# Ten FFN tiles ahead of the experts instead of twelve, sums through a PSUM bank

## The chip, the cores and the metric

The kernel runs on one core of a Trainium2 chip, in one launch. The metric is the device time of one execution in microseconds; of several runs the median is taken. The core has TensorE (PE in the profile, its weight loads PEld), VectorE (DVE), ScalarE (ACT), GpSimd (POOL) and SyncE (SP), each with its own queue of instructions in order, and they wait for each other on semaphores. All matrix products go to PSUM, which has eight banks of 512 fp32 columns on 128 partitions.

## The reference

A pre-norm decoder layer on x of 32 sequences x 64 rows x 256, that is 2048 rows or 16 tiles of 128. Linear attention and cross attention come first; the change lies in the FFN. There every row gets a shared FFN of width 352 and the two best of eight experts of width 176:

```python
x = x + linear_attention(_layernorm(x))
x = x + cross_attention(_layernorm(x), ctx)
xf = _layernorm(x)
weights, indices = top_k(softmax(xf @ gate_w.T), 2)      # weights over their sum
out = sum over the two experts e: weight_e * (silu(xf @ w_gate[e]) * (xf @ w_up[e])) @ w_down[e]
sh = silu(xf @ shw_gate) * (xf @ shw_up) @ shw_down
x = x + out + sigmoid(xf @ shgate_w) * sh
```

## The kernel before, in words

A tile is 128 rows. The attention loop works on 16 tiles in a software pipeline; its last tiles are drained by hand among the first shared FFN tiles. Every product of the FFN is three fp32r matmuls (high times high, high times low, low times high; `product`, L833), for which ScalarE writes the high half of an operand and VectorE the low one.

**A shared tile t.** TensorE transposes x_send (`transpose_sx`, L840); ScalarE writes s_xh, VectorE s_xl (`shared_x_low`, L1646). Then `shared_gate` and `shared_up` (12 matmuls), tanh on ScalarE (L1189), two VectorE steps (`s_gg` L1652, `s_h` L1657, together `shared_h`), three transposes (`transpose_sh`, L877), the split into s_hh (L1194) and s_hl (`sh_low`, L1662), nine matmuls (`shared_down`) and the addition to x_all (`residual3`, L1669). There is one down bank, DN, so `shared_down(t)` waits for `residual3(t-1)`.

**Routing.** VectorE ranks the rows in two batches, BATCHES = tiles 0 to 9 and 10 to 15. GpSimd then sends each tile by two indirect DMAs (`send`, L514) to rows in DRAM that are sorted by expert. Sends are paced by waits on s_h or e_h.

**The experts.** 39 slots of 128 sorted rows. SyncE loads slot i to xs (L410); the first FULL_SLOTS = 13 slots need batch 0 alone (semaphore sent0), and slots 4 to 11 have a clearing write behind each (L404). For slot i TensorE does `transpose_slots`, `gate_up` (6 matmuls), `transpose_h` (L972) and `expert_down` (6 matmuls), of different slots in one turn of the loop. ScalarE weights the result into e_y (`copy_y`, L1264, a ring of four), and GpSimd scatters it to y_rows (`scatter_out`, L568).

**Order.** It is written out by hand for each engine. EARLY_SHARED = 12 shared tiles run ahead of the experts, four behind them. The first two late tiles are mixed with the last two expert products: gate and up of tile 12 come ahead of `expert_down(37)`, and those of tile 13 behind `expert_down(38)`.

**The end.** When all scatters have landed, SyncE loads y_rows back as eight yg pieces of 512 KB, two tiles each (L427). GpSimd adds the two rows of each (`sum_y`, L577), VectorE adds the sum to x_all (`combine`, L1815), SyncE stores (L434). All eight combines stand on VectorE behind `sh_low(15)` and ahead of `residual3(14)`:

```python
while t >= TILES and done < PAIRS:
    combine(done)
    done += 1
if t >= TILES:
    v.wait_ge(sm["comb_ready"], PAIRS)
residual3(t - 2)
```

## Time and profile before

| | us |
|---|---|
| median of 3 runs | 400.0 (398.87 to 400.84) |
| the profiled execution | 398.38 |
| its span (first to last instruction) | 396.6 |
| TensorE busy | 355.9 (90%) |
| VectorE, ScalarE, GpSimd busy | 279.8, 209.3, 229.1 |
| first and last `gate_up` of the experts | 273.49, 360.73 |
| start of the yg loads | 372.38 |

The times in the profile count from the start of the span. Busy time is that of instructions on the engine; idle time is put down to whoever released the instruction behind it. The granted clock is that of TensorE, 1.00 for 2.4 GHz and 0.50 for 1.2 GHz. A duration is from start to end of one instruction; neighbours on an engine overlap a little, so their starts can lie closer together.

### The profile page before, as it was taken

To read this page: it belongs to the slowest core of one execution; us is meant where nothing else is said; L and a number is where in the kernel's file an instruction comes from. 1 tells how busy PE (TensorE), PEld (TensorE's weight loads), DVE (VectorE), ACT (ScalarE), POOL (GpSimd) and SP (SyncE) were. 2 spreads that over 40 slices of the span, in tenths; PEclk is the share of its full clock that TensorE was granted. 3 is DMA by queue.
4 is the path that set the end of the run, shared out by engine and by line. 5 is a ranking of instruction groups with operands and counts; after the bars stand their busy time and mean duration, and the time that the engine had idled before them with its cause. 6 is when DMAs were issued, how large, how long until landed. Compare 5 with 4: busy or idle time off the path is not lost.

```text
span 396.6 us, 11864 instructions
## 1 busy us (share of the span) xinstructions
PE 355.9 (90%) x3858; PEld 303.9 (77%) x3858; DVE 279.8 (71%) x904; ACT 209.3 (53%) x546; POOL 229.1 (58%) x263
## 2 busy tenths in 40 slices
PE   7789999999999999999986986999789999999932
PEld 5566777878778787787775886888679999998832
DVE  2757787777877778777886668976556676775575
ACT  2235657567575675756755533332446666565410
POOL 1247677886668866688655545444534444443293
PEclk9999999999999999999999899999999999999995
DMA  7922102221011210220000012123554444432493
GB/s 225 376 74 59 33 30 61 57 61 29 34 57 57 57 25 33 57 57 15 2 2 29 28 35 76 65 85 108 153 176 136 135 122 124 132 111 69 137 395 132
DMA packets 22013, 36.15 MB, mean 91 GB/s; under 512 B 2928, under 2 KB 15856, under 8 KB 21968
## 3 DMA queue, kind: packets, MB, share of 16 engines
q1 hardware_dynamic: 18128, 25.59, 21.1%
q0 software_dynamic: 3408, 9.39, 6.6%
q10 hardware_dynamic: 432, 0.59, 0.5%
q8 instruction: 25, 0.41, 0.4%
q14 instruction: 20, 0.16, 0.1%
HBM read 22.88 MB, written 12.69 MB: 90 GB/s over the span
## 4 chain that ended last, share of the span: by engine, by line
PE 64%; DVE 13%; ACT 9%; issue 7%; DMA 3%; POOL 2%; another core or an unknown queue 1%; ACTq 0%; SPq 0%; DVEq 0%; POOLq 0%
PE ps L833 22%; PE ps L601 8%; PE ps L730 4%; PE ps L648 4%; PE ps L702 4%; PE ps L677 3%; PE ps L610 3%; PE ps L667 3%; PE ps L635 2%; PE ps L972 2%; PE ps L957 2%; ACT w_hi L1089 2%; ACT q L1045 2%; PE ps L663 2%; ACT x_send L1092 2%
## 5 line engine op out<-in xcount | busy, mean ns | idle before, releaser
L568 POOL DMA_INDIRECT y_rows<-e_y,out_row x39 | 37.4, 959 | 49.3 <-ACT e_y L1264 47.1
L514 POOL DMA_INDIRECT xs_rows<-x_send,pos x32 | 31.1, 972 | 26.8 <-DVE s_h L1657 14.9
L497 POOL TENSOR_TENSOR w_lo<-w_stage,w_hi 128x852 f32 (+1 forms) x14 | 27.9, 1995 | 20.9 <-ACT w_hi L1089 19.8
L483 POOL TENSOR_TENSOR bias_t<-alibi,key_off 128x1024 f32<-128x1024 f32 x16 | 37.8, 2361 | 0.0
L490 POOL TENSOR_TENSOR sc<-sc,smax 128x1024 f32<-128x1024 f32 x16 | 30.4, 1901 | 6.7 <-DVE smax L1407 6.7
L601 PE MATMUL ps<-wkv,xn1T 128*128 128x512 f32 x64 | 31.7, 618 | 0.5 <-ACT xn1T L1081 0.5
L1743 DVE SCALAR_TENSOR_TENSOR e_gg<-e_th,ps 128x176 f32<-128x176 f32 x39 | 13.1, 337 | 26.2 <-ACT e_th L1253 23.1
L833 PE MATMUL ps<-w_hi,xh 128*128 x78 | 27.0, 346 | 1.3 <-issue 1.0
L456 POOL TENSOR_TENSOR st<-mv,eps 128x1 f32<-128x1 f32 x32 | 6.9, 216 | 35.6 <-DVE mv L1390 23.1
L833 PE MATMUL ps<-w_hi,s_xh 128*128 128x352 f32 x64 | 22.0, 343 | 6.1 <-DVE s_xl L1646 5.4
L833 PE MATMUL ps<-w_hi,s_hh 128*128 128x256 f32 (+1 forms) x48 | 15.6, 325 | 12.4 <-DVE x_all L1669 11.2
L833 PE MATMUL ps<-w_hi,e_hh 88*128 x78 | 25.2, 323 | 0.8 <-DVE e_hl L1754 0.7
L833 PE MATMUL ps<-w_lo,xh 128*128 x78 | 25.3, 324 | 0.0
L833 PE MATMUL ps<-w_hi,xl 128*128 x78 | 25.2, 323 | 0.0
L1264 ACT ACTIVATE e_y<-ps,id_w 128x256 f32<-128x256 f32 x39 | 18.5, 474 | 11.6 <-PE ps L833 9.5
L1253 ACT ACTIVATE e_th<-ps 128x176 f32<-128x176 f32 x39 | 12.4, 317 | 22.1 <-PE ps L833 18.5
L833 PE MATMUL ps<-w_hi,e_hl 88*128 x78 | 21.8, 280 | 0.0
L833 PE MATMUL ps<-w_lo,e_hh 88*128 x78 | 21.8, 280 | 0.0
L1401 DVE TENSOR_TENSOR sc<-ps,bias_t 128x1024 f32<-128x1024 f32 x16 | 19.5, 1218 | 2.1 <-remote 2.1
L833 PE MATMUL ps<-w_hi,s_xl 128*128 128x352 f32 x64 | 20.7, 324 | 0.0
L833 PE MATMUL ps<-w_lo,s_xh 128*128 128x352 f32 x64 | 20.7, 323 | 0.0
L730 PE MATMUL ps<-xw_last,o2T 128*128 128x256 f32 x64 | 18.9, 419 | 1.9 <-ACT o2T L1076 0.3
(223 smaller groups left out, 1164.7 us busy)
## 6 DMA issues: line engine op xcount, KB each, us to landing
w_stage<-in_w_ffn_dram SPq DMA_DIRECT2D x14, 426.0 KB, 3.3
xs<-xs_rows SPq DMA_DIRECT2D x39, 130.5 KB
yg<-y_rows SPq DMA_DIRECT2D x8, 512.0 KB, 7.5
ctxT<-in_ctxT_dram SPq DMA_DIRECT2D x16, 128.0 KB, 2.2
out_dram<-x_all SPq DMA_DIRECT2D x7, 256.0 KB, 3.6
x_all<-in_x_dram SPq DMA_DIRECT2D x1, 1280.0 KB, 10.6
xs_rows<-zeros SPq DMA_DIRECT2D x9, 130.5 KB, 7.0
y_rows<-e_y,out_row POOLq DMA_INDIRECT x39
```

Of the source, the lines that this page charges most:

```text
L483: nc.gpsimd.tensor_tensor(bias_t[:, :].rearrange("p (h k) -> p h k", h=HEADS), alibi[:, :].rearrange("p (h k) -> p h k", h=HEADS), ko, ALU ...
L490: nc.gpsimd.tensor_tensor(v, v, spread(smax[:, :].rearrange("p (h o) -> p h o", o=1), 2, S), ALU.subtract).then_inc(sm["sub_ready"], 1)
L497: nc.gpsimd.tensor_tensor(w_lo[:, cols], w_stage[:, half, :], w_hi[:, cols].bitcast(F32), ALU.subtract).then_inc(sm["w_lo_ready"], 1)
L514: nc.gpsimd.indirect_dma_start(out=xs_d[:, :], out_offset=bass.IndirectOffsetOnAxis(ap=pos[:, t, r:r + 1], axis=0), in_=x_send[:, t, :], i ...
L568: nc.gpsimd.indirect_dma_start(out=y_d[:, :], out_offset=bass.IndirectOffsetOnAxis(ap=out_row[:, i:i + 1], axis=0), in_=e_y[:, q, :], in_o ...
L601: mm = T.matmul(ps[:, A2, :], xn1T[:, k, :], wkv[:, k, :], start=(k == 0), stop=(k == KC - 1))
L648: mm = T.matmul(ps[:, A1, 0:D], oT[:, k, :], wo[:, k, :], start=(k == 0), stop=(k == KC - 1))
L702: mm = T.transpose(ps[:, B0 + b // 4, (b % 4) * P:(b % 4 + 1) * P], sc[:, b * P:(b + 1) * P], ident[:, :])
L730: mm = T.matmul(ps[:, A3, 0:D], o2T[:, k, :], xwo[:, k, :], start=(k == 0), stop=(k == KC - 1))
L833: mm = T.matmul(out_ap, lhs, rhs[rows, cols], start=st, stop=en)
L1264: A.activation(e_y[:, q, :], ps[:, ED + q % 2, 0:D], ACT.Copy, scale=id_w[:, i, 1:2]).then_inc(sm["e_y_ready"], 1)
L1401: V.tensor_tensor(sc[:, :].rearrange("p (j c) -> p j c", j=4), ps[:, B0:B3 + 1, 0:256], bias_t[:, :].rearrange("p (j c) -> p j c", j=4), A ...
```

## The change

- BATCHES is tiles 0 to 10 and 11 to 15. FULL_SLOTS follows: 15.
- EARLY_SHARED is 10: six shared tiles are behind the experts.
- On GpSimd each send comes one step earlier: send(1) stands ahead of rstd3(14), send(4) ahead of rstd3(15), and send(t) from 5 on waits for s_h(t-2) instead of s_h(t-1). Tiles 12 to 15 are sent behind the first four e_h (before: 13 to 15 behind the first three).
- `transpose_sx(t+1)` stands between gate and up of tile t, and VectorE does `shared_x_low(t+1)` between `shared_gg(t)` and `shared_gu(t)`, into which `shared_h` is split.
- At the end of the experts the x of tile 10 is transposed and split in slot 37. Then come gate of tile 10, `transpose_h(38)`, the last two `expert_down`, and only then up of tile 10.
- ScalarE copies each of GpSimd's sums into the PSUM bank LG (`sum_to_bank`, one bank, so copy k waits for combine k-1), and `combine` reads it there. Each combine now follows the residuals of its two tiles, and they are spread over the turns t = 12 to 17 (MIDDLE_SUMS, END_SUMS). In turn 12 ScalarE's copy of sum 0 comes behind `sh_high(11)` and ahead of tanh(13).

The diff, without the semaphore's name and the helpers that are only split:

```diff
--- before.py
+++ after.py
@@ -38,9 +38,11 @@
 REGION = B * S + P
 ZERO_ROW = NE * REGION
 ROW = D + 5
-BATCHES = ((0, 10), (10, 6))
+BATCHES = ((0, 11), (11, 5))
 DRAIN_SHARED = 3
-EARLY_SHARED = 12
+EARLY_SHARED = 10
+MIDDLE_SUMS = {14: (2,), 15: (4,)}
+END_SUMS = {12: (0,), 13: (1,), 14: (3,), 15: (5,), 16: (6,), 17: (7,)}
 FULL_SLOTS = (2 * BATCHES[0][1] * P - NE * (P - 1) + P - 1) // P
 PAIRS = TILES // 2
 
@@ -548,17 +550,20 @@
             rstd3(TILES - 3)
             send(0, 0)
             subtract_max(TILES - 1)
+            send(1, 0)
             rstd3(TILES - 2)
-            send(1, 0)
+            send(2, 0)
             pool.wait_ge(sm["s_hl_ready"], 2)
-            send(2, 0)
+            send(3, 0)
+            pool.wait_ge(sm["s_h_ready"], 3)
+            send(4, 0)
             rstd3(TILES - 1)
             for b, (t0, n) in enumerate(BATCHES):
-                for t in range(max(t0, 3), min(t0 + n, EARLY_SHARED + 1)):
-                    pool.wait_ge(sm["s_h_ready"], t)
+                for t in range(max(t0, 5), min(t0 + n, EARLY_SHARED + 2)):
+                    pool.wait_ge(sm["s_h_ready"], t - 1)
                     send(t, b)
-            for t in range(EARLY_SHARED + 1, TILES):
-                pool.wait_ge(sm["e_h_ready"], t - EARLY_SHARED)
+            for t in range(EARLY_SHARED + 2, TILES):
+                pool.wait_ge(sm["e_h_ready"], t - EARLY_SHARED - 1)
                 send(t, 1)
 
             def scatter_out(i, q):
...
@@ -928,13 +929,14 @@
             shared_gate(3, 1)
             shared_down(2, 0, A1)
             transpose_x3(15)
+            transpose_sx(4)
             shared_up(3, 1)
-            transpose_sx(4)
             router(15)
             for t in range(DRAIN_SHARED + 1, EARLY_SHARED):
-                shared_gate_up(t, t % 2)
+                shared_gate(t, t % 2)
                 if t + 1 < EARLY_SHARED:
                     transpose_sx(t + 1)
+                shared_up(t, t % 2)
                 transpose_sh(t - 1, (t - 1) % 2)
                 if t == DRAIN_SHARED + 2:
                     pe.wait_ge(sm["logits_ready"], TILES)
@@ -990,40 +992,44 @@
             shared_down(EARLY_SHARED - 2, 0)
             transpose_sh(EARLY_SHARED - 1, 1)
             expert = {}
-            for i in range(SLOT_TILES + 2):
+            for i in range(SLOT_TILES):
                 p = i % 2
-                late = EARLY_SHARED + i - SLOT_TILES
-                if i < SLOT_TILES:
-                    expert[i] = expert_of(i)
-                    gate_up(i, p, expert[i])
-                else:
-                    if i > SLOT_TILES:
-                        expert_down(i - 2, p, expert[i - 2])
-                    pe.wait_ge(sm["e_h_ready"], i - 1)
-                    pe.wait_ge(sm["e_hl_ready"], i - 1)
-                    shared_gate_up(late, late % 2)
+                expert[i] = expert_of(i)
+                gate_up(i, p, expert[i])
                 if i == 0:
                     shared_down(EARLY_SHARED - 1, 1)
                 if i == 2:
                     pe.wait_ge(sm["x3_ready"], EARLY_SHARED)
                     pe.wait_ge(sm["pos_ready"], 2)
-                if 1 <= i <= SLOT_TILES:
+                if i >= 1:
                     transpose_h(i - 1, 1 - p)
                 if i + 2 < SLOT_TILES:
                     transpose_slots(i + 2, (i + 2) % 4)
-                if i >= SLOT_TILES - 1:
+                if i == SLOT_TILES - 2:
                     pe.wait_ge(sm["e_xl_ready"], SLOT_TILES)
-                    transpose_sx(late + 1)
-                if i > SLOT_TILES:
-                    transpose_sh(late - 1, (late - 1) % 2)
-                if 2 <= i <= SLOT_TILES:
+                    transpose_sx(EARLY_SHARED)
+                if i >= 2:
                     expert_down(i - 2, p, expert[i - 2])
+
+            last = SLOT_TILES - 1
+            shared_gate(EARLY_SHARED, 0)
+            transpose_sx(EARLY_SHARED + 1)
+            transpose_h(last, last % 2)
+            expert_down(last - 1, (last - 1) % 2, expert[last - 1])
+            expert_down(last, last % 2, expert[last])
+            shared_up(EARLY_SHARED, 0)
+            shared_gate(EARLY_SHARED + 1, 1)
+            transpose_sx(EARLY_SHARED + 2)
+            shared_up(EARLY_SHARED + 1, 1)
+            transpose_sh(EARLY_SHARED, 0)
             pe.wait_ge(sm["e_y_ready"], SLOT_TILES)
             for t in range(EARLY_SHARED + 2, TILES + 2):
                 if t < TILES:
-                    shared_gate_up(t, t % 2)
+                    shared_gate(t, t % 2)
                 if t + 1 < TILES:
                     transpose_sx(t + 1)
+                if t < TILES:
+                    shared_up(t, t % 2)
                 if t - 1 < TILES:
                     transpose_sh(t - 1, (t - 1) % 2)
                 shared_down(t - 2, t % 2)
@@ -1276,28 +1282,34 @@
             slots_high(0, 0)
             slots_high(1, 1)
             sh_high(EARLY_SHARED - 1, 1)
-            for i in range(SLOT_TILES - 3):
-                experts(i, i % 4, i >= 1, i >= 2, True)
-            for i in range(SLOT_TILES - 3, SLOT_TILES + 2):
-                late = EARLY_SHARED + i - SLOT_TILES
-                if i > SLOT_TILES:
-                    copy_y(i - 2, (i - 2) % 4)
-                if i < SLOT_TILES:
-                    expert_tanh(i, i % 2)
-                else:
-                    shared_tanh(late, GT + late % 2)
-                if i <= SLOT_TILES:
-                    h_high(i - 1, (i - 1) % 2)
-                if i + 2 < SLOT_TILES:
-                    slots_high(i + 2, i % 2)
-                if i >= SLOT_TILES - 1:
-                    shared_x_high(late + 1, (late + 1) % 2)
-                if i > SLOT_TILES:
-                    sh_high(late - 1, (late - 1) % 2)
-                if i <= SLOT_TILES:
-                    copy_y(i - 2, (i - 2) % 4)
-            for t in range(EARLY_SHARED + 2, TILES + 1):
-                shared(t, 0, TILES)
+            for i in range(SLOT_TILES):
+                experts(i, i % 4, i >= 1, i >= 2, i + 2 < SLOT_TILES)
+                if i == SLOT_TILES - 2:
+                    shared_x_high(EARLY_SHARED, 0)
+            last = SLOT_TILES - 1
+            shared_tanh(EARLY_SHARED, GT)
+            h_high(last, last % 2)
+            shared_x_high(EARLY_SHARED + 1, 1)
+            copy_y(last - 1, (last - 1) % 4)
+            copy_y(last, last % 4)
+
+            def sum_to_bank(k):
+
+                act.wait_ge(sm["ysum_ready"], k + 1)
+                wait(act, sm["comb_ready"], k)
+                A.activation(ps[:, LG, :].rearrange("p (n d) -> p n d", n=2), yg[:, k, :, 0, :], ACT.Copy).then_inc(sm["ycopy_ready"], 1)
+
+            for t in range(EARLY_SHARED + 1, TILES + 2):
+                if t < TILES:
+                    shared_tanh(t, GT + t % 2)
+                if t + 1 < TILES:
+                    shared_x_high(t + 1, (t + 1) % 2)
+                for k in MIDDLE_SUMS.get(t, ()):
+                    sum_to_bank(k)
+                if t - 1 < TILES:
+                    sh_high(t - 1, (t - 1) % 2)
+                for k in END_SUMS.get(t, ()):
+                    sum_to_bank(k)
 
         @block.vector
         def _(v):
@@ -1647,15 +1659,22 @@
                                 s_xh[:, p, :, :].rearrange("p c t -> p (c t)").bitcast(F32), ALU.subtract).then_inc(sm["s_xl_ready"], 1)
 
 
-            def shared_h(t, p, gate, up):
+            def shared_gg(t, gate):
                 v.wait_ge(sm["s_th_ready"], t + 1)
+                wait(v, sm["s_h_ready"], t)
                 V.scalar_tensor_tensor(out=s_gg[:, :], in0=s_th[:, :], scalar=1.0, in1=ps[:, gate, 0:HS],
                                        op0=ALU.add, op1=ALU.mult).then_inc(sm["s_gg_ready"], 1)
+
+            def shared_gu(t, p, up):
                 v.wait_ge(sm["s_gg_ready"], t + 1)
                 v.wait_ge(sm["s_up_mm"], t + 1)
                 wait(v, sm["hT_mm"], t - 1)
                 V.scalar_tensor_tensor(out=s_h[:, p, :], in0=s_gg[:, :], scalar=sg4[:, bass.ds(t, 1)], in1=ps[:, up, 0:HS],
                                        op0=ALU.mult, op1=ALU.mult).then_inc(sm["s_h_ready"], 1)
+
+            def shared_h(t, p, gate, up):
+                shared_gg(t, gate)
+                shared_gu(t, p, up)
 
             def sh_low(t, p, bank=HT):
                 v.wait_ge(sm["s_hh_ready"], t + 1)
@@ -1670,10 +1689,10 @@
 
             def shared(t):
 
-                if t < EARLY_SHARED:
-                    shared_h(t, t % 2, GT + t % 2, UP + t % 2)
+                shared_gg(t, GT + t % 2)
                 if t + 1 < EARLY_SHARED:
                     shared_x_low(t + 1, (t + 1) % 2)
+                shared_gu(t, t % 2, UP + t % 2)
                 if t - 1 >= DRAIN_SHARED:
                     sh_low(t - 1, (t - 1) % 2)
                 if t - 2 >= DRAIN_SHARED:
@@ -1801,38 +1820,37 @@
             residual3(EARLY_SHARED - 1)
             for i in range(1, SLOT_TILES):
                 experts(i)
-            shared_x_low(EARLY_SHARED, 0)
-            shared_h(EARLY_SHARED, 0, GT, UP)
+                if i == SLOT_TILES - 2:
+                    shared_x_low(EARLY_SHARED, 0)
             h_low(SLOT_TILES - 1, (SLOT_TILES - 1) % 2)
             shared_x_low(EARLY_SHARED + 1, 1)
-            shared_h(EARLY_SHARED + 1, 1, GT + 1, UP + 1)
+            shared_gg(EARLY_SHARED, GT)
+            shared_gu(EARLY_SHARED, 0, UP)
+            shared_gg(EARLY_SHARED + 1, GT + 1)
             shared_x_low(EARLY_SHARED + 2, 0)
+            shared_gu(EARLY_SHARED + 1, 1, UP + 1)
             sh_low(EARLY_SHARED, 0)
 
             def combine(k):
-                v.wait_ge(sm["ysum_ready"], k + 1)
-                v.wait_ge(sm["x3_ready"], min(2 * k + 2, TILES - 2))
-                V.tensor_tensor(x_all[:, 2 * k:2 * k + 2, :], yg[:, k, :, 0, :], x_all[:, 2 * k:2 * k + 2, :], ALU.add
-                                ).then_inc(sm["comb_ready"], 1)
-
-            combined = {17: 7}
-            done = 0
+                v.wait_ge(sm["ycopy_ready"], k + 1)
+                v.wait_ge(sm["x3_ready"], 2 * k + 2)
+                V.tensor_tensor(x_all[:, 2 * k:2 * k + 2, :], ps[:, LG, :].rearrange("p (n d) -> p n d", n=2), x_all[:, 2 * k:2 * k + 2, :],
+                                ALU.add).then_inc(sm["comb_ready"], 1)
+
             for t in range(EARLY_SHARED + 2, TILES + 2):
                 if t < TILES:
-                    shared_h(t, t % 2, GT + t % 2, UP + t % 2)
+                    shared_gg(t, GT + t % 2)
                 if t + 1 < TILES:
                     shared_x_low(t + 1, (t + 1) % 2)
+                for k in MIDDLE_SUMS.get(t, ()):
+                    combine(k)
+                if t < TILES:
+                    shared_gu(t, t % 2, UP + t % 2)
                 if t - 1 < TILES:
                     sh_low(t - 1, (t - 1) % 2)
-                while t >= TILES and done < PAIRS:
-                    combine(done)
-                    done += 1
-                if t >= TILES:
-                    v.wait_ge(sm["comb_ready"], PAIRS)
                 residual3(t - 2)
-                while done < combined.get(t, 0):
-                    combine(done)
-                    done += 1
+                for k in END_SUMS.get(t, ()):
+                    combine(k)
 
 
 def kernel(**inputs):
```

## Rows read from the trace of the kernel before

**Rows 1.** The page's part 4: shares of the chain that ended last, by engine.

```profile
PE 64%; DVE 13%; ACT 9%; issue 7%; DMA 3%; POOL 2%; another core or an unknown queue 1%; ACTq 0%; SPq 0%; DVEq 0%; POOLq 0%
```

**Rows 2.** TensorE's waits in the whole span: who for, us in all, times, longest.

```profile
PE ps L833 <- DVE x_all L1669: 11.2, 2, 11.0
```

**Rows 3.** The chain in order of time from 364 us: start, us, what.

```profile
369.84 2.40 DMA y_rows<-e_y,out_row
...
373.23 6.11 DMA yg<-y_rows
...
385.29 1.27 DVE x_all L1815
...
393.95 0.42 DVE x_all L1669
```

**Rows 4.** Stretches: length, busy PE, PEld, DVE, ACT, POOL (xinstructions); clock, DMA share, GB/s.

```profile
273.50:298.65 25.15, 21.13 (x142) 18.48 (x140) 14.26 (x64) 11.11 (x34) 11.25 (x12) 1.00 0.48 146
298.65:361.80 63.15, 63.15 (x471) 61.67 (x470) 44.46 (x206) 39.20 (x116) 28.06 (x30) 1.00 0.40 122
373.20:376.00 2.80, 2.80 (x23) 2.78 (x23) 2.45 (x6) 0.88 (x4) 0.00 (x0) 1.00 0.93 294
376.00:379.00 3.00, 2.69 (x21) 2.49 (x20) 1.94 (x5) 1.01 (x3) 2.54 (x2) 1.00 1.01 397
```

**Rows 5.** Timeline, TensorE: start, us, line, operation, idle time before it and releaser.

```profile
217.23 0.48 PE L738 MATMUL ps<-ident,xn 128*128 128x128 f32 x2 [3.08 <-DVE sc L1401]
...
260.78 0.43 PE L833 MATMUL ps<-w_hi,s_xh 128*128 128x352 f32 x1 [0.84 <-DVE s_xl L1646]
...
264.43 0.32 PE L833 MATMUL ps<-w_hi,s_xh 128*128 128x352 f32 x1
...
267.97 0.32 PE L833 MATMUL ps<-w_hi,s_xh 128*128 128x352 f32 x1
...
271.29 0.60 PE L957 MATMUL ps<-ident,xs 128*128 128x128 f32 x4
...
273.49 0.41 PE L833 MATMUL ps<-w_hi,xh 128*128 x1
...
363.97 0.40 PE L833 MATMUL ps<-w_hi,s_xh 128*128 128x352 f32 x1 [0.86 <-DVE s_xl L1646]
...
391.58 0.55 PE L833 MATMUL ps<-w_hi,s_hh 128*128 128x256 f32 x1 [11.03 <-DVE x_all L1669]
```

**Rows 6.** Timeline, ScalarE, VectorE and GpSimd (POOL).

```profile
225.20 1.09 ACT L1059 ACTIVATE prT<-ps 128x512 f32<-128x512 f32 x2 [0.28 <-PE ps L702]
...
259.81 0.58 DVE L1657 SCALAR_TENSOR_TENSOR s_h<-s_gg,sg,ps 128x352 f32<-128x352 f32 x1
...
260.67 0.96 POOL L514 DMA_INDIRECT xs_rows<-x_send,pos  x1 [2.44 <-DVE s_h L1657]
...
368.58 0.96 POOL L568 DMA_INDIRECT y_rows<-e_y,out_row  x1 [3.22 <-ACT e_y L1264]
...
376.10 2.54 POOL L577 TENSOR_TENSOR yg<-yg 128x512 f32<-128x512 f32 x2 [5.29 <-DMA yg<-y_rows]
```

**Rows 7.** Timeline, SyncE's DMA queue.

```profile
265.99 10.46 SPq L410 DMA_DIRECT2D xs<-xs_rows  x5
...
372.38 3.79 SPq L427 DMA_DIRECT2D yg<-y_rows  x8
```

**Rows 8.** Stretches of 1 us after TensorE's gap in the drain.

```profile
217.00:218.00 1.00, 0.77 (x5) 0.80 (x6) 0.96 (x2) 0.26 (x1) 0.00 (x0) 0.73 0.00 0
...
220.00:221.00 1.00, 1.00 (x4) 0.78 (x3) 0.00 (x0) 0.64 (x1) 0.33 (x1) 0.57 0.00 0
```

**Rows 9.** Single lines: ns of one (min/median/max), first and last start, shapes.

```profile
L577 POOL TENSOR_TENSOR yg<-yg x8: 1256/1496/2922, 376.1 to 388.1; 128x512 f32<-128x512 f32 x8
...
L1815 DVE TENSOR_TENSOR x_all<-yg,x_all x8: 677/1208/1748, 380.6 to 390.3; 128x512 f32<-128x512 f32 x8
...
L1401 DVE TENSOR_TENSOR sc<-ps,bias_t x16: 1215/1217/1223, 32.2 to 215.9; 128x1024 f32<-128x1024 f32 x16
```

5 lines of the change are left out of this document (1 added, 4 removed).

## The prediction, made before the changed kernel ran

> **What bounds the kernel now.** I read the chain of waits first. TensorE carries 64% of it and VectorE 13% [rows 1], so what counts is where TensorE stands still. The list of its waits gives one large item: 11.0 us for a write of x_all on VectorE [rows 2]. The chain from 364 us on shows where that is: the last scatter of expert rows needs 2.40 us to land, the loads of yg carry 6.11 us, GpSimd's sums and VectorE's combines of 1.27 us follow, and the last residual starts at 393.95 [rows 3]. So after 380.5 us TensorE has only the down product of tile 15 left; that starts at 391.58, because residual3(14) stands on VectorE behind all eight combines. Before that TensorE sets the pace: it is busy all of 298.65 to 361.80, and 21.13 of 25.15 us in the first experts [rows 4]. A whole shared tile costs it 3.54 us (264.43 to 267.97), and the experts begin at 273.49 [rows 5].
>
> **1. Two shared tiles move behind the experts.** Tiles 10 and 11 leave the front: 2 x 3.54 = 7.1 us of TensorE. At the end they stand in the time in which the y rows are scattered, loaded and summed, where 11.0 us are idle. That is the cover.
>
> **2. What the front gives for it.** The experts need slot 0, whose load waits for the whole of batch 0. That batch had tiles 0 to 9, its last tile sent from 260.67 on (right behind s_h(8), which starts at 259.81 and takes 0.58), and the first load was issued at 265.99 [rows 6, 7]. Now send(10) belongs to it. Its wait is moved one s_h earlier, so it too hangs on s_h(8). Three small terms move s_h(8):
> - send(1) is now ahead of rstd3(14) on GpSimd. Two indirect DMAs (0.96 us each [rows 6] and a gap of 0.3) put that rstd some 0.7 us later. Queued behind it on ScalarE are ln3_norm(14) and then the prT copy at 225.20, before which ScalarE had only 0.28 us of idle time [rows 6]: +0.5 us, and TensorE, which waits for the copy, passes it on. send(4) ahead of rstd3(15) costs 0.3 more, which the slot table on VectorE covers; uncovered it would be another 0.3.
> - shared_x_low(t+1) now stands ahead of gu(t). TensorE's gates come about half a microsecond earlier (its waits here were for s_xl, 0.84 us for tile 9 [rows 5]), but VectorE is full in this stretch, so s_h(8) comes one s_xl later: +0.35.
> - Routing of eleven and five tiles, a table of 15 and 24 slots: between -0.2 and +0.1; I take -0.1.
>
> Together +0.75: the load of slot 0 goes out at about 266.75. How long it takes to land is not visible, since TensorE came to it late; the transposes at 271.29 bound it above by 5.3 us, the third yg load's 6.11 us [rows 3] is a loaded queue. With four loads queued at 266 I take 2.6 us: slot 0 at 269.4, slot 1 at 270.6. TensorE has run out by then: gate(9) at 260.65, then 3.4 us, done at 264.1. So it stands 5.3 us, and with that idles away most of the 7.1 us.
>
> **3. The clock in that gap.** Before, TensorE stood 3.08 us up to 217.23 [rows 5], waiting for VectorE, and the granted clock then went to 0.50 (1.2 GHz). The mean of 0.73 for 217 to 218 puts the fall at 217.5, that of 0.57 for 220 to 221 the return at 220.9: 3.4 us, half of it lost, 1.7 us [rows 8]. I expect the same here: shared_down(8) and the transposes run at 1.2 GHz until about 273, and gate_up(0) starts at 273.4 against 273.49. The front gains nothing. If the clock stays up it gains 1.3 to 1.7; if slot 0 lands 2 us later it loses 2. The Trainium skill ("TensorE: Matmul & The Clock Gate", section "Why this matters for your kernels") speaks against such a gap: it wants no idle gaps between bursts of matmuls, since each returns the clock to half rate. By that rule the moved work would cost the 1.7 us that the sum already has.
>
> **4. The experts.** 39 slots at 2.13 us do not change. Four sends instead of three now stand ahead of scatter_out(0) on GpSimd, the last behind e_h(3): scatter 0 goes out at some 289 instead of 286.3. It is waited for by copy_y(4) at 294; with 2.40 us to land that is covered by about 1.7 us, and uncovered would cost that difference. The loads of slots 13 and 14 no longer wait for batch 1, which had long been sent. Zero, so gate_up(38) ends at 361.8 as before.
>
> **5. Last expert products first.** Before, TensorE stood 0.86 us for s_xl(12), and down(38) came only after gate and up of tile 12, so the last two scatters left at 368.58 (3.22 us of idle before it) and 369.84 [rows 3, 5, 6]. Now x of tile 10 is split during slot 37. The order is down(36), gate(10) from 362.8, transpose_h(38), down(37), down(38) at 365.2 to 366.0 (ScalarE's tanh(10) is in front of h_high(38), 0.45 us, counted). copy_y(38) ends at 366.5; the scatters leave at 365.85 and 367.1. That is 2.7 us earlier, so the yg loads are issued at 369.7 instead of 372.38 [rows 7], and TensorE keeps working.
>
> **6. The end, stepped through.** TensorE: up(10), gate(11), up(11), sh(10) to 369.6; tiles 12 to 14 at 3.54 us would end at 380.2, down(15) near 387. Into this come the sums. yg(0) lands 3.7 us after its issue (372.38 to 376.10 [rows 6, 7]): 373.4. GpSimd adds it in 1.26 us (the least of its eight; the largest is 2.92 [rows 9]): 374.7. Then sum_to_bank(0) on ScalarE. Queued behind it are tanh(13) and x_high(14), and on VectorE behind combine(0) are gg(13) and x_low(14); TensorE's gate(14) waits for the latter. Free, tanh(13) would start at 374.2; it starts at 375.3, x_low(14) ends at 376.9 and gate(14) slips only 0.2 us. The copy itself is not in the trace. ScalarE's nearest is 128x512 from PSUM, two in 1.09 us [rows 6]; I take 0.57, with 0.5 and 0.7 as ends. The Trainium skill ("VectorE: DVE Perf Modes", section "The TRN2 errata") lists 224 cycles plus one per element at 1.2 GHz for a ScalarE operation with an SBUF source: an estimate of 0.61 us, which is 0.04 us more for each copy and would leave the time as it is.
>
> The combine with one PSUM source is not there either: 1.217 us for 1024 columns on one side, and on the other the present one at its least, 0.677 for 512 [rows 9]. I take 0.68 and expect none of the 1.27 us spacing, which appears only where GpSimd's and VectorE's SBUF sums alternate. Bounds: 0.61 to 1.27.
>
> From 375.3 VectorE is the bound. A shared tile costs it 2.45 us (six instructions [rows 4]); it has left three tiles, one s_hl and one residual: 7.35 + 0.65 + 0.4 = 8.4, and eight combines 5.4: 13.8 us, so 389.1. TensorE's down(15) (387.5 at the latest) and the other yg loads (1.5 us apart, the last at 384) are hidden under it. After the last VectorE write the old end took 396.6 - 394.37 = 2.2 us. Both stores of pair 7 now wait for combine(7), and one issue costs 3.79/8 = 0.47 [rows 7]: 389.1 + 2.2 + 0.45 = 391.75.
>
> **The sum.** End of the experts unchanged (0.0), tail 396.6 to 391.75, 0.15 for waits between engines that I did not see: span 391.9, -4.7 us. The profiled execution took 398.38 us, 1.78 around its span: 393.7. The median of the runs is 400.0, 0.4% above that execution; scaled the same way, 395.3.
>
> **Rivals.**
> - *The gap costs no clock and slot 0 lands fast.* For: the 2.6 us of landing are a choice, 2.0 would do. Against: 5.3 us is longer than the 3.08 that dropped the clock. gate_up(0) at 271.8: -1.6, so 393.6. Chance 0.17.
> - *The first sum comes late.* ScalarE and VectorE both stand in order behind yg(0). If that load takes the 6.11 us of the third one instead of 3.7 [rows 3], or combines cost 1.0, 2.4 us pass straight to the end: 397.7, or 398.5 with a late slot 0. For: VectorE has no slack from there on. Together with all cases within 0.5%: 0.14.
> - *Slower: the clock stays low through the first experts.* With the gap at 264, gate_up(0) to (3) start cold; there TensorE already has 4.0 us of gaps in 25.15 [rows 4], each could keep it down. Each us at 1.2 GHz costs half a us, so it turns a loss once more than 9.4 us beyond those counted run low. For 14 us: -4.7 + 7 = +2.3, so 402.3. The Trainium skill ("TensorE: Matmul & The Clock Gate", section "HAM oscillation") describes such a clock, lost again at every wait for DMA. Against: the full clock was back 3.7 us after work resumed [rows 5, 8], and it was 1.00 throughout the old gaps of the experts [rows 4]. Chance 0.07.
> - *It doesn't do what it says:* the sums could still be last if transfers bound the end. 4.2 MB of loads and 2.1 MB of stores after 370.3, at the 397 GB/s of 376 to 379 [rows 4], are 16 us: 386.3, below 389.1. Chance 0.02, about 397.5.
>
> The forecast itself has 0.60, with its own range of 394.0 to 397.2. With the rivals and bounds (-1.6 for the front, +1.3 each for combine and landing) 8 times in 10 it is 392.6 to 398.9. About 0.5%, 2 us, is what a measurement of this kernel tells from no change: faster by more 0.79, within 0.14, slower 0.07.
>
> **What will show it.** TensorE idle 4 to 6 us near 264 to 269, waiting for xs, with a clock of 0.50 behind it; the first expert product at 273.4 +- 1.5; the last two scatters under 1.5 us apart, near 367; the yg loads at 369.7; ScalarE standing 1 to 2 us before its first copy of yg; combines near 0.68 and GpSimd's sums near 1.3; no idle time over 2 us on TensorE after 362 and its clock at 1.00 to the end. I am wrong if the gap is under 3 us, if the experts end after 364, or if VectorE is idle by more than 2 us after 376.

## The result, and the profile after

| | kernel before | changed kernel |
|---|---|---|
| median of 20 runs each, us | 400.46 (398.68 to 402.18) | 398.06 (396.44 to 400.36) |
| ratio, 95% interval | | 0.9948 [0.9928, 0.9968] |
| profiled execution: time, span, us | 398.38, 396.6 | 398.82, 397.0 |

The change gains 2.4 us, 0.5%. Ratios, here and below, leave out the few runs that lie over 1.5% above the fastest of their kernel, so they can differ from the quotient of two medians. The forecast was 395.3 us, 4.7 less than the 400.0 of before. The two profiled spans are even 0.4 us apart in the other direction, so the profile after has to be read for where 4.7 us went. The prediction's sum can be laid on three marks: ScalarE's first tanh of an expert, its last (slot 38), and the end of the span.

| us | first tanh | first to last | last to end | span |
|---|---|---|---|---|
| before | 274.74 | 87.26 | 34.60 | 396.6 |
| forecast (gate_up(0) at 273.4) | 274.65 | 87.26 | 29.9 to 30.0 | 391.9 |
| changed | 274.65 | 91.86 | 30.49 | 397.0 |

The first tanh came when it was forecast, and the end is nearly as long as forecast. All but 0.6 of the 5.1 us lie in the middle column, for which the working had zero.

TensorE's list of waits over the whole span (who for, us in all, times, longest) has no 11.0 us for x_all any more [rows 2], and a new head:

```profile
PE ps L959 <- DMA xs<-xs_rows: 7.0, 3, 4.5
```

On TensorE's timeline the standing ahead of slot 0 is the first of three (start, us, line, operation, idle time before it and its releaser):

```profile
268.71 0.66 PE L959 MATMUL ps<-ident,xs 128*128 128x128 f32 x2 [4.49 <-DMA xs<-xs_rows]
...
272.51 0.64 PE L838 MATMUL ps<-w_hi,xh 128*128 x1
...
284.04 0.42 PE L838 MATMUL ps<-w_hi,xh 128*128 x1 [1.86 <-DVE xl L1757]
...
298.12 0.49 PE L959 MATMUL ps<-ident,xs 128*128 128x128 f32 x2 [2.22 <-DMA xs<-xs_rows]
```

With each of the three standings that are 1.8 us and longer the granted clock falls, the first time while TensorE still stands (stretches, columns as in [rows 4]; the clock is the third number from the end):

```profile
268.00:274.00 6.00, 5.03 (x21) 4.67 (x22) 1.94 (x7) 1.31 (x4) 0.00 (x0) 0.50 0.25 71
...
276.00:284.00 8.00, 5.92 (x42) 5.29 (x40) 4.04 (x17) 2.28 (x7) 5.74 (x6) 1.00 0.51 162
284.00:292.00 8.00, 7.48 (x33) 6.70 (x34) 3.73 (x18) 3.33 (x10) 4.47 (x5) 0.57 0.45 133
292.00:298.00 6.00, 3.62 (x25) 3.10 (x23) 3.54 (x15) 2.82 (x9) 2.24 (x3) 1.00 0.49 162
298.00:304.00 6.00, 5.88 (x31) 5.55 (x32) 2.00 (x9) 2.20 (x6) 0.96 (x1) 0.72 0.49 143
```

Before, the same stretch ran at 1.00 [rows 4]. At 0.57 over 8 us and 0.72 over 6, up to 8 x 0.43 + 6 x 0.28 = 5.1 us of full-clock time were lost, and the middle column grew by 4.6. What TensorE stood for goes back to ScalarE and to SyncE's queue:

```profile
283.06 0.38 ACT L1254 ACTIVATE xh<-ps 128x256 fp32r<-128x256 f32 x1 [2.46 <-remote]
...
366.51 0.32 ACT L1259 ACTIVATE e_th<-ps 128x176 f32<-128x176 f32 x1 [0.52 <-PE ps L838]
```

```profile
290.52 0.30 SPq L412 DMA_DIRECT2D xs<-xs_rows  x1
...
294.56 0.33 SPq L412 DMA_DIRECT2D xs<-xs_rows  x1
```

ScalarE stood 2.46 us, and at 284.61 another 1.17, for nothing that the profile can name. The load of slot 9 went out at 294.56, 4.0 us after slot 8's (2.6 in the kernel before), and TensorE waited for it at 298. But the kernel before has nearly the same standing of ScalarE at the same place, behind the third tanh:

```profile
280.52 0.32 ACT L1253 ACTIVATE e_th<-ps 128x176 f32<-128x176 f32 x1 [2.08 <-remote]
```

There no wait of TensorE in the experts was longer than 0.89 us (for a load, at 292.84), and the clock held. What is new in the changed kernel is that TensorE stood for 1.86 and 2.22 us.

The end, against [rows 3, 6]: the last scatter, the yg loads, GpSimd's sums, the first copy to the bank, the first and last combine, and TensorE's last product:

```profile
372.09 0.96 POOL L573 DMA_INDIRECT y_rows<-e_y,out_row  x1 [0.33 <-issue]
...
378.28 9.00 POOL L582 TENSOR_TENSOR yg<-yg 128x512 f32<-128x512 f32 x7 [5.22 <-DMA yg<-y_rows]
```

```profile
374.60 2.90 SPq L429 DMA_DIRECT2D yg<-y_rows  x6
```

```profile
379.59 0.60 ACT L1300 ACTIVATE ps<-yg 128x512 f32<-128x512 f32 x1 [2.07 <-POOL yg L582]
```

```profile
380.23 0.69 DVE L1837 TENSOR_TENSOR x_all<-ps,x_all 128x512 f32<-128x512 f32 x1 [1.73 <-ACT ps L1300]
...
393.68 0.69 DVE L1837 TENSOR_TENSOR x_all<-ps,x_all 128x512 f32<-128x512 f32 x1
```

```profile
391.81 0.36 PE L838 MATMUL ps<-w_hi,s_hh 128*128 128x256 f32 x1 [0.61 <-DVE x_all L1688]
```

Seven sums take 1.29 us each, a combine 0.69 instead of 1.27, and TensorE stands 0.61 us where it stood 11.03 [rows 5].

### The profile page after: what moved, and what is told of

It reads as the page before. It is cut to its first block, busy times and chain, and to the rows that moved or that the text cites. A ratio compares the mean times of both kernels' runs of the same rounds, so it can differ in the third digit from the quotient of the medians.

```text
span 397.0 us, 11888 instructions
## 1 busy us (share of the span) xinstructions
PE 361.5 (91%) x3858; PEld 309.8 (78%) x3858; DVE 274.6 (69%) x904; ACT 213.1 (54%) x554; POOL 226.4 (57%) x263
## 4 chain that ended last, share of the span: by engine, by line
PE 52%; issue 27%; ACT 8%; DMA 5%; DVE 3%; SPq 3%; POOL 1%; ACTq 1%; another core or an unknown queue 0%; DVEq 0%; POOLq 0%
PE ps L838 17%; PE ps L606 7%; PE ps L735 3%; PE ps L653 3%; PE ps L615 3%; PE ps L682 3%; PE ps L707 3%; PE ps L672 2%; PE ps L640 2%; PE ps L959 2%; ACT w_hi L1095 2%; DMA bkv<-in_bkv_dram 2%; PE ps L974 2%; PE ps L668 2%; ACT q L1051 2%
## 5 line engine op out<-in xcount | busy, mean ns | idle before, releaser
L838 PE MATMUL ps<-w_hi,xh 128*128 x78 | 28.1, 360 | 2.4 <-DVE xl L1757 2.1
L838 PE MATMUL ps<-w_hi,e_hh 88*128 x78 | 26.2, 336 | 0.3 <-DVE e_hl L1773 0.3
L838 PE MATMUL ps<-w_hi,xl 128*128 x78 | 26.4, 338 | 0.0
L838 PE MATMUL ps<-w_lo,xh 128*128 x78 | 26.3, 338 | 0.0
L838 PE MATMUL ps<-w_hi,s_xh 128*128 128x352 f32 x64 | 22.8, 356 | 3.0 <-DVE s_xl L1658 3.0
L1757 DVE TENSOR_TENSOR xl<-ps,xh 128x256 fp32r<-128x256 f32 x39 | 16.0, 411 | 11.4 <-ACT xh L1254 11.4
L959 PE MATMUL ps<-ident,xs 128*128 128x128 f32 x78 | 16.1, 290 | 7.0 <-DMA xs<-xs_rows 7.0
L1254 ACT ACTIVATE xh<-ps 128x256 fp32r<-128x256 f32 x39 | 14.6, 374 | 13.1 <-PE ps L959 10.6
## 6 DMA issues: line engine op xcount, KB each, us to landing
x_all<-in_x_dram SPq DMA_DIRECT2D x1, 1280.0 KB, 10.5
```

What stands on the lines that cost most here:

```text
L838: mm = T.matmul(out_ap, lhs, rhs[rows, cols], start=st, stop=en)
L959: mm = T.transpose(ps[:, EX + p, k * P:(k + 1) * P], xs[:, q, k * P:(k + 1) * P], ident[:, :])
L1254: A.activation(xh[:, p, :, :].rearrange("p c t -> p (c t)"), ps[:, EX + p, 0:D], ACT.Copy).then_inc(sm["e_xh_ready"], 1)
L1757: V.tensor_tensor(xl[:, p, :, :].rearrange("p c t -> p (c t)"), ps[:, EX + p, 0:D], xh[:, p, :, :].rearrange("p c t -> p (c t)").bitcast(F ...
```

## The experiments

Theories ahead of the runs: **A**, the standing at the front (the gap, from here on) costs clock and the falls in the experts follow from it; **B**, the four late sends hold up the experts' start; **C**, the batch of eleven makes the gap; **D**, the engines' own stalls, whose place is chance. The runs came on five chips. On three the kernel before took 393 to 394 us (I call them quick), on two 400 to 401 like the first (slow). Each ratio is against the kernel before on the same chip.

### The gap filled (twice), and the changed kernel beside it

```
+            pe.wait_ge(sm["s_h_ready"], EARLY_SHARED - 1)
+            keep_warm(LG, 9)
             pe.wait_ge(sm["slots_ready"], 1)
             transpose_slots(0, 0)
-            pe.wait_ge(sm["s_h_ready"], EARLY_SHARED - 1)
```

> The changed kernel with nine matmuls of zeros (0.42 us each at full clock, 3.8 us in all) put where TensorE stands 4.5 us for the rows of slot 0. Nothing waits for them. Theory A (the standing costs clock, and the slow start of the experts follows from it): granted clock 1.00 through 264 to 274, gate_up(0) at 271.5 (272.5 in the changed kernel), the last gate_up near 362 (365.2), time 0.985 to 0.990 of the kernel before. Theory B (the late sends hold up the start) and theory D (stalls of the engines' own instruction streams, whose place is chance): gate_up(0) up to 1 us earlier, but the last gate_up stays at 364 to 366 and the ratio at 0.992 to 0.996.

> The changed kernel itself, for its ratio and its profile on the same chip as the other experiments. Theory D (the slow start of its experts in the first profile, 5.5 us over 39 steady slots and a clock that fell twice more, is chance or this chip's): last gate_up comes about 4.5 to 6 us after the steady pace counted from gate_up(0), no clock under 0.9 after 280, ratio still 0.992 to 0.998. Theory A (the standing brings the later falls of the clock): falls again between 284 and 302 in the profile, ratio 0.993 to 0.997.

> The changed kernel with the nine matmuls of zeros in the gap, beside the changed kernel on one chip. Theory A: 2 to 4 us less than the changed kernel (0.5% to 1%). Theory D: at most the 1.7 us that the prediction worked out for the low clock in and behind the gap, 0.2% to 0.45% less.

> The changed kernel again, on one chip with the next three. On a chip on which the kernel before takes near 400 us (as on the first), ratio 0.993 to 0.997 and a mean clock over the runs of 0.967 to 0.976; on one on which it takes near 394, 0.988 to 0.992 and 0.982 to 0.995.

> The changed kernel with the gap filled by nine matmuls of zeros. Theory A (on the slower kind of chip the filled gap also spares later falls of the clock in the experts): 3.5 to 6 us under the changed kernel there, no fall of the clock after 276, mean clock over 0.985. Rival (the falls in the experts come from their own standings, whatever the gap): 2 to 3 us under it, as on the other kind of chip, falls of the clock in the experts all the same.

| | changed | gap filled |
|---|---|---|
| first quick chip | | 388.23, 0.9869 [0.9834, 0.9905] |
| second | 389.97, 0.9900 [0.9863, 0.9937] | 387.12, 0.9837 [0.9802, 0.9872] |
| third | 389.73, 0.9892 [0.9852, 0.9932] | 386.73, 0.9827 [0.9796, 0.9859] |

The filling, which computes nothing, is worth 2.9 and 3.0 us by the medians. The stretches of the changed kernel and of the filled one on the third chip show why:

```profile
264.00:276.00 12.00, 7.94 (x41) 7.56 (x42) 3.65 (x16) 2.02 (x6) 1.88 (x2) 0.72 0.28 77
276.00:304.00 28.00, 25.72 (x178) 23.25 (x177) 17.29 (x80) 15.27 (x46) 15.83 (x18) 1.00 0.59 174
```

```profile
264.00:276.00 12.00, 10.06 (x68) 8.76 (x67) 6.77 (x30) 4.26 (x13) 3.91 (x5) 1.00 0.40 118
276.00:304.00 28.00, 26.71 (x191) 24.81 (x189) 17.67 (x82) 15.99 (x48) 15.27 (x16) 1.00 0.57 170
```

The clock of 0.72 over 12 us is 3.4 us of full-clock time, but TensorE worked only from 268.00 on, where it is 0.65 over 8: 2.8 us at most. The price can be read more closely. From TensorE's first transpose of slot 0 to the first tanh it takes 5.7 to 6.0 us in the four profiles with the gap and 3.6 to 3.7 in the four with it filled, and in both TensorE resumes when the load lands. So the gap's clock costs some 2.0 to 2.4 us up to there, against the 1.7 of the prediction. Where the rest of the medians' 2.9 and 3.0 lies no profile shows. Here the changed kernel keeps 1.00 in the experts, with the gap unfilled, and from first to last tanh both kernels take the same (85.66 and 85.24). So A's second half, that the gap brings the later falls, does not hold on quick chips. The slow start of the first profile was seen on slow chips alone.

### Where the load of slot 0 stands: a first batch of ten

```
-BATCHES = ((0, 11), (11, 5))
+BATCHES = ((0, 10), (10, 6))
```

> The changed kernel with first batch of ten tiles and second of six (one line). The first load then waits for the send of tile 9 (259 us) and not for tile 10's (263.5). Theory C (the batch of eleven makes the gap, and with it the loss): the first load issued near 262, TensorE's gap under 1.5 us, gate_up(0) near 269.5, ratio 0.985 to 0.988. Theory B or D: the gap closes as well, but the experts' start gives it back by stalls and loads of the later slots that come late: last gate_up at 363 to 366, ratio 0.992 to 0.997.

> The changed kernel with a first batch of ten. By theory C, 6 us under the changed kernel, ratio 0.974 to 0.980 on either kind of chip. Rival (what the earlier start gains is given back in a start of the experts in which slots 13 and 14 now wait for the second batch, and in falls of the clock): 2 to 4 us under it.

383.44 us, 0.9741 [0.9712, 0.9769], and 382.71, 0.9740 [0.9704, 0.9777]: 7.0 us under the changed kernel on one chip (third), the best kernel of the study. The SyncE queue and TensorE in the second of these:

```profile
258.43 8.46 SPq L412 DMA_DIRECT2D xs<-xs_rows  x5
```

```profile
262.37 0.41 PE L959 MATMUL ps<-ident,xs 128*128 128x128 f32 x2 [1.16 <-DMA xs<-xs_rows]
```

and the changed kernel's queue on the same chip, whose TensorE stood 4.76 us:

```profile
265.31 9.35 SPq L412 DMA_DIRECT2D xs<-xs_rows  x5
```

Filling the gap gives 3.0; from the filled kernel to the batch of ten it is 388.23 - 383.44 = 4.8 on the first quick chip and 386.73 - 382.71 = 4.0 on the third. On the first their first loads went out at 262.95 and 258.15, 4.8 apart, but TensorE, which now stands 1.2 to 1.7 us instead of 4.5 to 4.8, got 3.7 and 4.0 us of it: by so much the first tanh is earlier (269.23 to 265.48, 269.20 to 265.17). Theory C has it: one tile in the batch costs some 4 us of waiting, and the gap that it opens costs 2 to 3 of clock on top. In both profiles the clock stayed at 1.00 through the standing that is left.

### The end alone, and the moved tiles alone

The first is the changed kernel with twelve early tiles and batches of ten and six as before, so with the new end, but also with the new order of the sends and of `transpose_sx` in the front. Its sums are placed late:

```
-EARLY_SHARED = 10
-MIDDLE_SUMS = {14: (2,), 15: (4,)}
-END_SUMS = {12: (0,), 13: (1,), 14: (3,), 15: (5,), 16: (6,), 17: (7,)}
+EARLY_SHARED = 12
+MIDDLE_SUMS = {}
+END_SUMS = {15: (0,), 16: (1, 2), 17: (3, 4, 5, 6, 7)}
```

> The changed end alone: twelve shared tiles ahead, batches of ten and six as in the kernel before, last expert products first, sums over a PSUM bank, the sums' places in the loops moved to the last turns. Front as in the kernel before: gate_up(0) 273.5, last gate_up 360.7. If the prediction's working of the end holds (yg loads at 369.7, sums 1.29 each, copy 0.60, combine 0.68, store 2.6 after the last) the span ends near 391.8, ratio 0.987. Theories A, B and C, by which the front is what loses, give 0.985 to 0.990 here; theory D gives 0.987 to 0.993, since the start of the experts varies with it too.

The second is the kernel before with `EARLY_SHARED = 10` and batches of eleven and five.

> The kernel before with only its two numbers changed: ten shared tiles ahead and six behind, batches of eleven and five. The end is the old one: last shared products before the last expert products, combines of 1.27 us from SBUF. By the prediction's working the 7.1 us of moved products lie in the 11.0 us in which TensorE stood, and the front gains nothing: ratio 0.998 to 1.002. Theories A and B: the experts end 2 to 4 us later, ratio 1.004 to 1.010. Theory C is not told apart from A here.

The end alone: 389.05 us, 0.9887 [0.9860, 0.9914], 4.8 us gained by the medians, as much as was forecast for the whole change. Behind its last tanh it takes 29.5 us, against 34.0 to 34.6 in the three profiles of the kernel before and 30.5 to 30.7 in the changed kernel. So the tiles that the change moves behind the experts cost about 1 us there, unless the sums' other places account for it. The moved tiles alone: 399.16, 1.0136 [1.0098, 1.0175], 5.3 us lost. TensorE and the queue in the latter:

```profile
271.16 0.66 PE L957 MATMUL ps<-ident,xs 128*128 128x128 f32 x2 [6.58 <-DMA xs<-xs_rows]
```

```profile
268.98 9.30 SPq L410 DMA_DIRECT2D xs<-xs_rows  x5
```

The experts begin at 277.32 (first tanh; 271.20 with the end alone), and behind the last tanh it takes 36.2 us against 34.0 to 34.6 in the kernel before, although TensorE still stands 5.5 us there. The two moved tiles were not free at the end. That they cost their time on VectorE, which also makes the combines, is likely but not shown.

The fronts can be compared from one mark, TensorE's product behind the prT copy in the drain, so that what differs ahead of it drops out. In the first profiles of before and after it is

```profile
226.43 1.13 PE L715 MATMUL ps<-v_bd,prT 128*64 128x34 f32 x32 [0.72 <-ACT prT L1059]
```

```profile
227.75 1.13 PE L720 MATMUL ps<-v_bd,prT 128*64 128x34 f32 x32 [0.72 <-ACT prT L1065]
```

| from this mark to the first tanh, us | |
|---|---|
| kernel before (3 profiles) | 48.3 |
| end alone | 47.0 |
| changed kernel (4, with the stalled one) | 46.9 to 47.0 |
| gap filled (4, with the stalled one) | 44.8 to 45.0 |
| batch of ten (2) | 41.5, 40.9 |
| old order of sends | 49.2 |
| moved tiles alone | 50.5 |

The end alone and the changed kernel have the same front time, with twelve and with ten tiles in it: what the two tiles would have taken is idled away or lost to the clock, as forecast. The 1.3 us under the kernel before come from the new orders.

### The order of the sends

> The changed kernel with GpSimd's order of sends as before the change (send(1) behind rstd3(14), the send of tile t waiting for the h of tile t, tiles 11 to 15 sent in the experts). By the trace of the kernel with only its tiles moved, the send of tile 10 goes out when tile 9's h is done, some 6 us later than in the changed kernel, and five sends stand ahead of the first scatter. The gap of TensorE grows from 4.5 to 9 us or more: ratio 1.003 to 1.012, 4 to 7 us over the changed kernel. If the gap were of little consequence (what is lost there being hidden later) it would stay within 0.3% of the changed kernel.

The pool's list of sends as in the kernel before: 390.54 us, 0.9940 [0.9910, 0.9970]; 0.6 us over the changed kernel, intervals overlapping (0.4% by the ratios). My expectation of 4 to 7 us was wrong: send(10) went out at 259.33 against 258.39 in the changed kernel on that chip, 0.9 us later and not 6. The gap grew to 6.85 us (4.54), and from the mark to the first tanh it is 2.2 us more; but the way to the mark is shorter, 7.9 us from the end of TensorE's wait in the drain against 8.9 to 9.0 in the profiles on quick chips with the new order of sends whose clock held there. The moved tiles alone start late for the same send: it waits for s_h(9) at 263.31 and goes out at 264.16, where in the changed kernel on the third quick chip, which reached the mark at the same time (226.8), it goes out at 260.33.

```
             for t in range(EARLY_SHARED + 2, TILES):
-                pool.wait_ge(sm["e_h_ready"], t - EARLY_SHARED - 1)
+                pool.wait_ge(sm["s_h_ready"], EARLY_SHARED)
                 send(t, 1)
```

> The changed kernel with a first batch of ten tiles, and the sends of tiles 12 to 15 not held back into the experts (they wait for the last early shared tile only). Theory B (the late sends stand ahead of the scatters and loads): first scatter 4 us earlier, startup of the experts 1.5 to 2.5 us shorter, ratio 0.966 to 0.971 (0.974 without it). Its rival: the eight writes meet the loads of slots 0 to 3 and the instructions' own fetches, gate_up(0) and (1) come 1 to 2 us later, ratio 0.974 to 0.980.

On the batch of ten: 384.89 us, 0.9788 [0.9748, 0.9828] (0.974 without it). From first to last tanh its profile takes 84.3 us, less than the 85.0 and 86.5 of the batch of ten, but the median is no shorter. Theory B would have gained 1 to 3 us; the times give it no support.

> A first batch of ten and four matmuls of zeros (1.7 us) in the 1.7 us in which TensorE still stands there. Where the clock held at 1.00 in that gap without them (as in the first profile of the batch of ten) they bring nothing, and up to 0.5 us is lost by their being in the way; where it fell, 1 to 3 us are gained.

384.42 us, 0.9776 [0.9743, 0.9810]: 1.7 us over the batch of ten, though intervals overlap. The gap of 1.2 us had cost no clock, and filling it brought nothing.

### The same stalls on a slow chip

To imitate what the first profile shows at 283 to 302, ScalarE is held up in the experts' turns 2, 5 and 8:

```
+                if i in (2, 5, 8):
+                    act.wait_ge(sm["s_gg_ready"], EARLY_SHARED)
+                    for n in range(5):
+                        A.activation(s_th[:, :], s_gg[:, :], ACT.Copy).then_inc(sm["oT_ready"], 1)
+                        act.wait_ge(sm["oT_ready"], TILES + 5 * (i // 3) + n + 1)
```

> The kernel before itself, for a profile on the chip of the other experiments. If its experts start as those of the other kernels did there, the loss over the steady pace from the first tanh to the last is 4 to 5 us (6.2 in the first profile) and the first tanh stands near 271.3, so that the front of the change gains or loses nothing within 0.5 us and its end gains 4.0 us, which is what the changed kernel showed (3.6 us).

> The changed kernel with ScalarE held up by five dependent copies (about 2.5 us) in each of the experts' turns 2, 5 and 8, as the first profile of the changed kernel showed it held up at 283, 290 and 301 us. Theory A2 (the standing at the front leaves TensorE's clock so that a later standing of 2 us brings it down again): a clock of 0.5 to 0.7 behind two of the three, and 6 to 9 us over the changed kernel. Theory D2 (a stall costs the same wherever it falls; the gap has nothing to do with it): as much over the changed kernel as the kernel before with the same stalls is over its own (3 to 6 us).

> The same three stalls in the changed kernel with its gap filled. Theory A2: the clock stays at 1.00 in the experts, 3 to 5 us over the kernel with the gap filled, so 4 to 6 us under the stalled changed kernel. Theory D2: only the 2.8 us of the gap's own clock lie between the two.

> The same three stalls in the kernel before. Theory A2: no fall of the clock, 3 to 5 us over the kernel before, ratio 1.008 to 1.013, and the change is then worth nothing or a loss beside it. Theory D2: the change keeps its 3.6 us under stalls.

Medians: changed 401.10 us, 0.9955 [0.9923, 0.9988]; gap filled 397.87, 0.9928 [0.9901, 0.9956]; kernel before 401.89, 1.0034 [1.0007, 1.0060]. The changed kernel, TensorE's second standing and the clock behind it, then the filled one:

```profile
285.48 0.42 PE L838 MATMUL ps<-w_hi,xh 128*128 x1 [1.94 <-DVE xl L1762]
```

```profile
284.00:292.00 8.00, 6.53 (x36) 6.33 (x37) 3.90 (x19) 4.29 (x12) 3.85 (x4) 0.79 0.52 149
...
296.00:304.00 8.00, 6.74 (x30) 6.52 (x31) 3.86 (x18) 4.34 (x14) 2.87 (x3) 0.57 0.46 138
```

```profile
283.30 0.43 PE L838 MATMUL ps<-w_hi,xh 128*128 x1 [1.93 <-DVE xl L1763]
```

```profile
284.00:292.00 8.00, 7.02 (x46) 5.74 (x44) 3.97 (x19) 5.08 (x14) 4.80 (x5) 1.00 0.53 166
...
296.00:304.00 8.00, 6.88 (x49) 6.42 (x48) 3.96 (x19) 6.17 (x17) 2.30 (x3) 1.00 0.47 139
```

The same standing of 1.9 us dropped the clock in one and not in the other, and first to last tanh took 94.2 and 90.8 us. That speaks for A. But the kernel before, with no gap ahead of its experts, also fell once, behind a standing of 1.94 us (0.85 over 284 to 292, 89.9 us), where A2 had no fall, and the ratios of the two changed kernels are only 0.3% apart, which is less than the gap's own clock explains. The sizes were missed by both theories: the stalls cost the kernel before 0.3%, not 3 to 6 us, and the changed kernel with them keeps 0.8% under the kernel before with them. Among the changed kernel's own runs of up to 402 us, those with a mean clock of 0.975 and more took 396.1 to 398.1, those with 0.971 and less 398.6 to 402.0. So a lower clock goes with a longer time; that the gap brings the falls is not shown.

### The kernel before again, and sends one tile ahead, on a slow chip

> The kernel before, for a profile beside those of the changed kernels. The changed kernel's first tanh of an expert stands at 271.8 and 273.7 in its two profiles on the faster kind of chip, and the end behind its last tanh is 30.6 long (34.6 before). If the front gains nothing, the first tanh stands here at 271 to 274 and the loss over the steady pace is 4.2 to 5, on a chip with the kernel before near 394; near 400 it is 274 to 277 and 6 to 7.

> A first batch of ten, with the sends of tiles 5 and up let go one tile earlier (the send of tile t waits for the h of tile t-2 and not t-1). The first load then goes out some 4 us earlier and TensorE's last 1.2 to 1.7 us of standing are gone: gate_up(0) up to 1.2 us earlier, 1 to 1.5 us under the kernel with the batch of ten alone. Rival: the send meets LayerNorm's and the routing's work on GpSimd and nothing is gained.

The two profiles of the kernel before from slow chips (399.71 and 400.91 us) took 87.65 and 87.54 us from first to last tanh, as the first one did. The batch of ten with `pool.wait_ge(sm["s_h_ready"], t - 2)`: 391.36 us, 0.9764 [0.9721, 0.9807], no better a ratio than that of the batch of ten alone (0.974, on quick chips), and TensorE has no wait for slot 0 left. Yet first to last tanh takes 90.1 us and the clock falls again (0.79 over 285 to 290), behind a standing of TensorE of 1.54 us. So on a slow chip the experts lose clock in a kernel without any gap ahead of them. ScalarE in the kernel before and in this one:

```profile
283.31 0.32 ACT L1253 ACTIVATE e_th<-ps 128x176 f32<-128x176 f32 x1 [2.03 <-remote]
284.77 0.38 ACT L1258 ACTIVATE e_hh<-ps 88x256 fp32r<-88x256 f32 x1 [1.14 <-remote]
```

```profile
279.83 0.47 ACT L1270 ACTIVATE e_y<-ps,id_w 128x256 f32<-128x256 f32 x1 [1.88 <-remote]
```

Laid side by side, the profiles show what goes with a fall in the experts. Of the eight from slow chips, the two with the gap open fell twice each, for 10.2 us in all each time; of the six without it two fell once, for 3.4 us. Every one of these six falls came with a standing of TensorE of 1.5 to 2.2 us; in the filled and stalled kernel standings of 1.93 and 1.68 us passed at 1.00. Where TensorE stood for less than 1.2 us in the experts (the kernel before on three slow chips, and all twelve profiles from quick chips, four of them with the gap) the clock never fell there. So the long standings in the experts are needed in all that was seen, and the gap is not. Whether a gap ahead makes a fall likelier stays open.

## Why the prediction was right and wrong

**1 and 2, the moved tiles and the gap: right.** The load of slot 0 went out at 266.94 (forecast 266.75), TensorE stood 4.49 us (5.3), slot 0 was transposed at 268.71 (269.4).

**3, the clock of the gap: right in kind, too small.** Predicted 1.7 us from the one earlier gap in that profile; the filled gap shows 2.0 to 2.4 up to the first tanh and 2.9 to 3.0 in the medians. That the first tanh fell on 274.65 to the digit is luck. Slot 0 landed 1.8 us after its issue, not 2.6, and in the drain the clock was low for 6.8 us (0.57 over 216 to 224) instead of the 3.4 of before (0.79), so that TensorE took 10.25 us from its wait there to the mark of the table above instead of 9.20; the other two profiles of the kernel before, with as long a low stretch, took 10.4 and 10.5. From the mark on the front gained 1.4 us. "The front gains nothing" holds for the moved tiles, not for the new orders beside them. What the sentence hid is how much was to be had: the same front with a batch of ten is 7 us better. I took the cover of 11.0 us at the end as the thing to check and gave the eleventh tile 0.75 us, the change in send(10)'s own time, without asking when send(9)'s load could have gone.

**4, the experts: the step that failed.** "39 slots at 2.13 us do not change ... Zero." They took 91.86 instead of 87.26 us, and the last gate_up started at 365.24, behind the 364 that the prediction had set as a sign of being wrong. The zero left out the clock: in that profile TensorE stood 1.86 and 2.22 us among the first ten slots, and 10.2 us of the experts ran at 1.2 GHz, 5.1 us of full-clock time. It was my slower rival's mechanism, at 0.07, which wanted more than 9.4 us of them. I argued against it with the full clock of the kernel before [rows 4], but there the 4.0 us of standings in 25 us were all single ones under 0.9 us. The total was reassuring; how long each standing would be in the new order I did not ask. The Trainium skill ("TensorE: Matmul & The Clock Gate", section "HAM oscillation") describes a kernel whose clock is lost again at each wait for DMA; this trace agrees in kind at 298.12, where 2.22 us for slot 9 go with 0.72 over 6 us, though the waits of its example are longer, some 3 to 5 us. Of the size in the median only an estimate is possible: it misses the forecast by 2.8 us, of which the end has 0.6, so some 2.2 us lie in the experts of a usual run, on a slow chip. The clocks of the 20 runs say that a usual run has such falls: their median is 0.972, which over 396 us is 22 us at 1.2 GHz, and the gap (6.8) and the drain (3.4 to 6.8) do not fill that. On quick chips the experts lost nothing (85.6 us, and 85.2 with the end alone), and there the change is worth 3.3 to 3.6 us. What stays open is why TensorE's standings grew past 1.8 us in the changed kernel on the slow chip, and whether the gap ahead of them had a part in the falls.

**5, the last expert products first: right.** Last scatter 5.6 us behind the last tanh (5.1 forecast), 1.28 us after the one before it, and the yg loads at 8.1 (7.7). The half microsecond is VectorE's: 1.35 us of idle time ahead of e_hl(38) that nothing explains.

**6, the end: right.** First sum 3.7 us after the first load (3.7), sums 1.29 (1.26), copies 0.60 (0.57; the Trainium skill, "VectorE: DVE Perf Modes", section "The TRN2 errata", gave an estimate of 0.61, and the trace agrees), combines 0.69 (0.68), and 2.6 us behind the last write (2.65). From first sum to last combine 16.1 us against 15.7. The whole end is 30.5 us, forecast 29.9. The kernel with the end alone bears it out: 29.5 us there, 4.5 to 5.1 less than before.

**The scale from one profiled run.** The profile of before was a quick one: span 396.6, where two more took 397.9 and 399.1. Scaling by the median put that right.

**The rival "first sum late"** did not occur; GpSimd started 3.7 us after the issue. Transfers were not the bound: TensorE stood 0.61 us for VectorE at the end.

## What to carry to other kernels

When work is moved out from in front of a load, the load's own condition sets the new start: ask for the last member of what it waits for, and what it would cost to have one fewer. Here one tile fewer in the batch was worth more than the whole change. The standing of 4.5 us cost its own length and then 2 to 3 us of clock, and nine matmuls of zeros in it gave those back; a standing of 1.2 us in the same place cost no clock. And a stretch that ran at full clock is no proof that it will when the work around it is reordered: look at the longest single wait in it, and ask what would make it longer.

## What was not expected of the hardware

The same kernel took 393 to 394 us on three chips and 400 to 401 on others, and part of the difference sits in fixed places. The plainest is in the drain, near 216 us. On all eight profiles of slow chips VectorE's last `sc` and ScalarE beside it stand there 2.0 and 2.5 to 2.7 us with "remote" as the reason, so that TensorE waits 3.0 to 3.1 us for them; in all twelve profiles of quick chips neither stands for "remote" there, and TensorE waits 1.0:

```profile
215.86 1.22 DVE L1401 TENSOR_TENSOR sc<-ps,bias_t 128x1024 f32<-128x1024 f32 x1 [2.06 <-remote]
```

The second place is at slots 2 to 4 of the experts. On seven of the eight profiles of slow chips ScalarE stands there for 1.1 to 2.5 us with "remote" or "issue" as the reason, in kernels whose experts begin up to 8 us apart (the eighth, the kernel before with added stalls, stands 1.3 and 1.9 us there with TensorE as the reason). From the third tanh to the fourth it is 4.80 to 6.22 us without added stalls, and 2.70 to 2.96 in all twelve profiles of quick chips. In these runs it goes with the place in the program and the chip, not with the time or with the work around it. What the engines stand for is not shown.
